# Attention scores kept in SBUF instead of computed twice, softmax sums on TensorE

## The reference

```python
xn = layernorm(x)                                        # over the 256 columns
score = einsum('bci,bcj->bij', ctx, xn) / sqrt(256)      # 64 x 256 x 256
score = softmax(score, axis=0)                           # over the 64 batches
x = x + einsum('bci,bij->bcj', ctx, score)
# then x + moe(layernorm(x)): 8 experts of 256-512-256, 2 chosen per token, gelu
```

## Time and profile before

| | |
|---|---|
| median of 3 runs | 813.24 us (811.27 to 814.58) |
| the profiled execution | 818.82 us, its span 817.0 us |
| busy share of the span | PE 91%, DVE 76%, POOL 66%, ACT 47% |
| stage 1, first to last maximum and on to stage 2 | 0 to 77 us |
| stage 2, to the first product with the reciprocal | 77 to 156 us |
| stage 3 | 156 to about 290 us |
| routing, then experts | about 290 to 346 us, then to the end |
| DMA | 137.20 MB, 174 GB/s to and from HBM over the span |

### The profile page before, as it was taken

One profiled execution on the slowest core, in us unless ns is written; L12 is line 12 of the kernel. 1 busy time (PEld: TensorE's weight loads), 2 busy tenths in 40 slices (PEclk: granted clock), 3 DMA queues, 4 the chain that ended last, 5 costly groups with the idle time before them and its releaser, 6 DMA issues. The chain is left out here.

```text
span 817.0 us, 22178 instructions
## 1 busy us (share of the span) xinstructions
PE 742.1 (91%) x5931; PEld 647.5 (79%) x5932; DVE 618.5 (76%) x1520; ACT 387.1 (47%) x716; POOL 538.5 (66%) x658
## 2 busy tenths in 40 slices
PE   6999999598999844499999999999979999999995
PEld 4777888477788734399999999999958999999995
DVE  5998999897999967786667676627467766767664
ACT  3554666375766751144444445414424444444441
POOL 4664777586888720657777777736677777777764
PEclk9999999798999955599999999979999999999998
DMA  7887876256888650445555555534355444444440
GB/s 217 259 258 233 242 234 203 88 172 207 268 270 270 228 199 0 103 141 159 183 163 186 167 181 179 160 114 132 104 167 143 152 146 134 132 139 130 139 113 1
DMA packets 82201, 137.20 MB, mean 168 GB/s; under 512 B 10075, under 2 KB 55140, under 8 KB 82032
## 3 DMA queue, kind: packets, MB, share of 16 engines
q0 software_dynamic: 23104, 68.43, 28.0%
q1 hardware_dynamic: 59056, 68.26, 26.8%
HBM read 94.56 MB, written 47.59 MB: 174 GB/s over the span
## 5 line engine op out<-in xcount | busy, mean ns | idle before, releaser
L1051 ACT ACTIVATE work<-psum,b1T 128x256 f32<-128x256 f32 x312 | 131.0, 471 | 259.3 <-PE psum L670 259.2
L670 PE MATMUL psum<-work,w1T_high 128*128 128x256 f16 x1248 | 213.1, 276 | 2.7 <-ACT work L1059 2.7
L693 PE MATMUL psum<-w2T_high,slots 128*128 x1248 | 210.2, 274 | 1.1 <-issue 1.1
L670 PE MATMUL psum<-work,w1T_low 128*128 128x256 f16 x624 | 172.3, 276 | 0.0
L693 PE MATMUL psum<-w2T_low,slots 128*128 x624 | 170.8, 274 | 0.0
L942 DVE CAST slots<-work 128x512 f16<-128x512 f32 x156 | 68.8, 441 | 118.6 <-ACT work L1051 118.4
L670 PEld LDWEIGHTS psum<-work,w1T_high 128*128 x1248 | 123.4, 99 | 18.7 <-issue 3.1
L693 PEld LDWEIGHTS psum<-w2T_high,slots 128*128 128x128 f16 x1248 | 119.2, 98 | 14.8 <-issue 1.8
L551 PE MATMUL psum<-slots,work 128*128 (+1 forms) x512 | 124.2, 393 | 7.1 <-ACT slots L981 6.5
L506 POOL DMA_INDIRECT slots<-rows_first,slots x86 | 89.4, 1039 | 60.5 <-DVE slots L903 34.6
L513 POOL DMA_INDIRECT rows_second<-slots x78 | 83.4, 1069 | 55.9 <-issue 34.7
(11 more groups left out here) (123 smaller groups left out, 1076.9 us busy)
## 6 DMA issues: line engine op xcount, KB each, us to landing
work<-in_ctx SPq DMA_DIRECT2D x96, 256.0 KB, 3.6
rows_first<-slots SPq DMA_DIRECT2D x32, 514.0 KB, 3.9
slots<-in_x SPq DMA_DIRECT2D x32, 256.0 KB, 3.8
work<-in_L_ffn_w SPq DMA_DIRECT2D x32, 256.0 KB, 3.2
work<-in_x SPq DMA_DIRECT2D x32, 256.0 KB, 3.1
slots<-rows_first,slots POOLq DMA_INDIRECT x86
rows_second<-slots POOLq DMA_INDIRECT x78
slots<-rows_second,slots POOLq DMA_INDIRECT x78, 3.7
```

Source lines behind the costliest of these rows:

```text
L670: mm = pe.matmul(h, w1T[pw][:, f, c, bass.ds(e * P, P)], xT[r2][:, (px * HC + c) * GROUP:(px * HC + c + 1) * GROUP], start=(c == 0 and px ...
L693: mm = pe.matmul(y, act16[r2][pa][:, f * GROUP + s * P:f * GROUP + (s + 1) * P], w2T[pw][:, f, bass.ds(e * DIM, DIM)], start=(f == 0 and p ...
L1051: last = act.activation(act32[r2][:, f * GROUP:(f + 1) * GROUP], psum[:, 2 + 2 * r2 + f // 2, (f % 2) * GROUP:(f % 2 + 1) * GROUP], ACT.Ge ...
```

## The change

The scores are computed once. ScalarE copies each pair's scores from PSUM into its slots, over the normalised x that TensorE has read, and VectorE takes the maximum from the same PSUM banks after that copy; the banks are now a ring of four pairs. Stage 2 has no products, ctx loads or transposes left: VectorE subtracts the maximum in SBUF, in place, ScalarE takes the exponential, and TensorE adds up by multiplying each batch's exponentials with the identity into PSUM bank 7. The reciprocal reads that bank. GpSimd does nothing in stage 2.

The host now hands over x and ctx as [row, batch, column], so that a pair is 2 KB in one piece for each partition (with 64 KB from one partition's to the next), and the expert weights, router weights and first bias already transposed. One block of 512 columns of weights is loaded, split by ScalarE and VectorE from SBUF for each pair.

```diff
@@ DMA queue (sync) @@
-            sp.wait_ge(s_setT, 1)
-            def load_exps(i, k, n):
+            def load_weights(i, k, n):
                 m, r = i + k, k % RING
-                sp.wait_ge(m_score, m + PAIRS - RING + 1)
-                sp.dma_start(ctx_ring[:, 2 * r:2 * r + 2, :], pair_of(ctx, m * 2)).then_inc(m_ctx_in[r], 16)
-                if k % 2 == 0:
...
+                after(sp, e_wlow, m - RING + 1)
+                sp.dma_start(stage[:, 2 * r:2 * r + 2, :].rearrange("p a b -> p (a b)"), weights_of(m, weights)).then_inc(e_w_in[r], 16)
@@ GpSimd: add_up and its loop are gone @@
@@ TensorE @@
+            def scores(i, k, n):
                 m, r = i + k, k % RING
                 pe.wait_ge(m_ctx_in[r], landed_at(i, k, RING))
-                after(pe, m_max, m - 1)
+                after(pe, m_max, m - RING + 1)
                 for j in range(2):
                     pe.wait_ge(m_q, m * 2 + j + 1)
...
-            pipeline(pe, PAIRS, RING, RING, 0, scores_exp)
+            def sum_up(i, k, n):
+                m = i + k
+                if isinstance(m, int) and m == 0:
+                    pe.wait_ge(m_max, PAIRS)
+                pe.wait_ge(e_exp, m + 1)
                 for j in range(2):
+                    mm = pe.matmul(psum[:, 7, :], ident[:], slot(m * 2 + j, 0, 2 * DIM), start=(isinstance(m, int) and m == 0 and j == 0),
+                                   stop=(isinstance(m, int) and m == PAIRS - 1 and j == 1))
@@ VectorE @@
                 if live(i, k, L_MAX, PAIRS):
-                    m, r2 = i + k - L_MAX, (k - L_MAX) % 2
-                    dve.wait_ge(m_score, m + 1)
-                    banks = psum[:, 2 * r2:2 * r2 + 2, :]
+                    m = i + k - L_MAX
+                    dve.wait_ge(m_kept, m + 1)
+                    banks = score_banks(k - L_MAX)
...
+            def differences(i, k, n):
                 if live(i, k, 0, PAIRS):
+                    m = i + k
+                    dve.wait_ge(m_kept, m + 1)
+                    dve.tensor_tensor(slot2(m * 2, 0, 2 * DIM), slot2(m * 2, 0, 2 * DIM),
                                       smax[:, 0:1, :].to_broadcast([P, 2, 2 * DIM]), ALU.subtract).then_inc(e_diff, 1)
+                if live(i, k, L_LOW, PAIRS):
+                    m, r = i + k - L_LOW, (k - L_LOW) % RING
+                    dve.wait_ge(e_whigh, m + 1)
+                    dve.scalar_tensor_tensor(weights_of(m, halves[1]), stage[:, 2 * r:2 * r + 2, :].rearrange("p a b -> p (a b)"), WSCALE,
+                                             weights_of(m, halves[0]), ALU.mult, ALU.subtract).then_inc(e_wlow, 1)
+            dve.wait_ge(e_sum, 1)
+            dve.reciprocal(ssum[:, 0:PROD_POOL], psum[:, 7, 0:PROD_POOL]).then_inc(e_recip, 1)
+            dve.reciprocal(ssum[:, PROD_POOL:], psum[:, 7, PROD_POOL:]).then_inc(e_recip, 1)
@@ ScalarE @@
             def queries(i, k, n):
+                if live(i, k, 0, PAIRS):
+                    m, r = i + k, k % RING
+                    act.wait_ge(m_norm, m + 1)
+                    for j in range(2):
+                        act.activation(slot(m * 2 + j, 0, DIM), slot(m * 2 + j, 0, DIM), ACT.Identity, bias=shift[:, r, j:j + 1],
+                                       scale=rstd[:, r, j:j + 1]).then_inc(m_q, 1)
+                if live(i, k, L_KEEP, PAIRS):
+                    m = i + k - L_KEEP
+                    wait_apart(act, m_score, m + 1)
+                    act.activation(slot2(m * 2, 0, 2 * DIM), score_banks(k - L_KEEP), ACT.Copy).then_inc(m_kept, 1)
+            pipeline(act, PAIRS, RING, RING, L_KEEP, queries)
...
+                act.wait_ge(e_w_in[r], landed_at(i, k, RING))
+                act.activation(weights_of(m, halves[0]), stage[:, 2 * r:2 * r + 2, :].rearrange("p a b -> p (a b)"), ACT.Copy, scale=WSCALE).then_inc(e_whigh, 1)
                 act.wait_ge(e_diff, m + 1)
                 act.activation(slot2(m * 2, 0, 2 * DIM), slot2(m * 2, 0, 2 * DIM), ACT.Exp, scale=SCORE_SCALE).then_inc(e_exp, 1)
```

More of the change, by code:

```diff
@@ L51 @@
 PR = 2 * DIM
-SUM_DVE = 128
+W_HALF = EXPERTS * HID * DIM // P
+W_STEP = 2 * W_HALF // (BATCH // 2)
 PROD_POOL = 320
@@ L130, in landed_at, with xattn_ffn @@
     return i * (16 // ring) + landed(k, ring)
-def xattn_ffn(nc, x, ctx, router_w, w1, b1, w2, b2, out):
-    w1_rows = w1.rearrange("e f h -> (e f) h")
-    w2_rows = w2.rearrange("e h f -> (e h) f")
+def xattn_ffn(nc, x, ctx, router_w, b1, weights, b2, out):
     out_rows = out.rearrange("b c l -> (b c) l")
@@ L153, in xattn_ffn @@
         slots3 = slots[:].rearrange("p (b w) -> p b w", w=ROW)
-        w1T = [sb(f"w1T_{p}", [P, FC, HC, EXPERTS * P], F16) for p in ("high", "low")]
-        w2T = [sb(f"w2T_{p}", [P, FC, EXPERTS * DIM], F16) for p in ("high", "low")]
+        halves = [sb(f"weights_{p}", [P, 2 * W_HALF], F16) for p in ("high", "low")]
+        w1T = [t[:, 0:W_HALF].rearrange("p (f h w) -> p f h w", f=FC, h=HC) for t in halves]
+        w2T = [t[:, W_HALF:].rearrange("p (f w) -> p f w", f=FC) for t in halves]
         smax = sb("smax", [P, 3, 2 * DIM])
-        sums = smax[:, 1:3, :]
-        ssum = sums[:, 0, :]
+        ssum = smax[:, 1, :]
         choice = smax[:, 0, 0:ROUNDS * BATCH].rearrange("p (r b) -> p r b", r=ROUNDS)
@@ L201, in slot2, with weights_of, score_banks @@
             return slots3[:, bass.ds(b, 2), first:first + n]
[L203 to L206 removed]
+        def weights_of(m, t):
+            return t[:, bass.ds(m * W_STEP, W_STEP)]
+        def score_banks(k):
+            return psum[:, 2 * (k % RING):2 * (k % RING) + 2, :]
         def pair_of(dram, b):
[L209 removed]
+            return dram[:, bass.ds(b, 2), :]
         s_zero = sem("s_zero")
@@ L378, in _ @@
         def _(sp):
-            sp.dma_start(rw_in, router_w).then_inc(s_rw_in, 16)
-            sp.dma_start(work[0:EXPERTS, 16:18, :].rearrange("e a b -> e (a b)"), b1).then_inc(s_b1_in, 16)
+            sp.dma_start(rwT[:].rearrange("p h e -> p (h e)"), router_w).then_inc(s_rw_in, 16)
+            sp.dma_start(b1T[:].rearrange("p e f -> p (e f)"), b1).then_inc(s_b1_in, 16)
             def load_scores(i, k, n):
@@ L391, in _ @@
             pipeline(sp, PAIRS, RING, 2 * RING, L_CTX, load_scores)
-            sp.wait_ge(s_setT, 1)
-            def load_exps(i, k, n):
+            def load_weights(i, k, n):
                 m, r = i + k, k % RING
-                sp.wait_ge(m_score, m + PAIRS - RING + 1)
-                sp.dma_start(ctx_ring[:, 2 * r:2 * r + 2, :], pair_of(ctx, m * 2)).then_inc(m_ctx_in[r], 16)
-                if k % 2 == 0:
[L401 to L405, removed]
+                after(sp, e_wlow, m - RING + 1)
+                sp.dma_start(stage[:, 2 * r:2 * r + 2, :].rearrange("p a b -> p (a b)"), weights_of(m, weights)).then_inc(e_w_in[r], 16)
+            pipeline(sp, PAIRS, RING, RING, 0, load_weights)
             def attend(i, k, n):
@@ L539, in _ @@
             pe.wait_ge(s_const, 1)
[L540 to L553, removed]
@@ L555, in scores_max @@
-            def scores_max(i, k, n):
+            def scores(i, k, n):
                 m, r = i + k, k % RING
                 pe.wait_ge(m_ctx_in[r], landed_at(i, k, RING))
-                after(pe, m_max, m - 1)
+                after(pe, m_max, m - RING + 1)
                 for j in range(2):
                     pe.wait_ge(m_q, m * 2 + j + 1)
[L561 to L569, removed]
-                for j in range(2):
[L571 to L583, removed]
@@ L584, in _ @@
-            pipeline(pe, PAIRS, RING, RING, 0, scores_exp)
+                    for h in range(HC):
+                        mm = pe.matmul(psum[:, 2 * r + j, h * DIM:(h + 1) * DIM], ctx_ring[:, 2 * r + j, h * P:(h + 1) * P], slot(m * 2 + j, 0, DIM),
+                                       start=True, stop=True)
+                mm.then_inc(m_score, 1)
+            pipeline(pe, PAIRS, RING, RING, 0, scores)
+            def sum_up(i, k, n):
[3 more added lines that the diff above has]
+                pe.wait_ge(e_exp, m + 1)
+                for j in range(2):
+                    mm = pe.matmul(psum[:, 7, :], ident[:], slot(m * 2 + j, 0, 2 * DIM), start=(isinstance(m, int) and m == 0 and j == 0),
+                                   stop=(isinstance(m, int) and m == PAIRS - 1 and j == 1))
+                if isinstance(m, int) and m == PAIRS - 1:
+                    mm.then_inc(e_sum, 1)
@@ L757, in _ @@
-            pipeline(dve, PAIRS, RING, RING, L_LOW, exponentials)
-            dve.wait_ge(e_sumv, PAIRS)
-            dve.wait_ge(e_sump, PAIRS)
-            dve.tensor_tensor(ssum, ssum, sums[:, 1, :], ALU.add).then_inc(e_total, 1)
-            dve.wait_ge(e_total, 1)
-            dve.reciprocal(ssum[:, 0:PROD_POOL], ssum[:, 0:PROD_POOL]).then_inc(e_recip, 1)
-            dve.reciprocal(ssum[:, PROD_POOL:], ssum[:, PROD_POOL:]).then_inc(e_recip, 1)
+                if live(i, k, L_LOW, PAIRS):
[3 more added lines that the diff above has]
```

(18 more changed lines are left out.)

64 lines of the change are left out of this document (11 added, 53 removed).

## The result

The changed kernel takes 816.40 us (median of 10 runs, 814.85 to 818.18) against 813.87 (median of 10, 811.27 to 815.56): a ratio of 1.0033, 95% interval 1.0018 to 1.0048. It is slower by 2.5 us or 0.3%, clear of the noise, half of the 5.2 us that were forecast, and within the 0.5% that I called no change: that outcome had 0.27, and the likelier one, slower by more, 0.57. The profiled execution took 818.18 us, with a span of 816.4.

A forecast was written before the change was run, and what follows sets the result against it. The prediction took stage 1 to be bound by a round trip through the engines, not by one engine. Stage 1 +20.3, stage 2 -15.1 and stage 3 0 gave +5.2 on 813.2, so 818.4 us; range 806 to 832.

The forecast's parts named there:

- both large terms: Stage 1 was to grow by 20.3 us and stage 2 to shrink by 15.1 us.
- The order on ScalarE sets stage 1: Stage 1: copy waits behind the next pair's normalising, so the period is 2.69 us instead of 2.04; +20.3 us in all.
- the copy: Stage 1: ScalarE's added copy of 128x1024 from PSUM per pair, taken as 1.05 us, bounds 1.0 and 1.2.
- VectorE sets stage 2's pace, TensorE its end: Stage 2: VectorE 1.74 and TensorE 1.73 us a pair, TensorE without slack for its late start; stage -15.1 us.
- The sums start at half clock: Start of stage 2's sums: after 5.6 us idle TensorE runs at half clock, losing 1.7 to 3.5 us, taken as 2.5.
- Stage 3 starts as before: Start of stage 3: TensorE again at half clock after some 3.3 us waiting; 0, with a gain of at most 1.7 us.
- The halt is not part of the median: Stage 3: VectorE's 5.0 us stop for late ctx taken as absent from the median; rival that change ends it: 813.4, 0.10.
- the clock did not fall in stage 1: Rival for stage 1: idle gaps halve TensorE's clock over half the pairs, giving 834 us; chance 0.10.
- The loads are no slower for their pitch: Rival on loads with 64 KB between partitions: twice as slow, they cost 33 us in stage 3, 851 us; chance 0.04.
- The sum on TensorE ran as said: Rival for stage 2: the sum's products take twice the 1.73 us, stage grows by 55, 874 us; chance 0.02.
- the first rival: Stage 1: the order on ScalarE doesn't bind, the period stays at 2.04 us, 799.2 us in all; chance 0.08.

The follow-up runs named there:

- the second profile of the kernel before: The kernel before, unchanged, run once more for its profile: 813.24 us in this execution.
- the half sum: The changed kernel with the second batch of each pair left out of the sums in stage 2: 810.82 us in a single execution.
- the 24 products: The changed kernel with 24 small unused identity products on TensorE between the last scores and the first sum: 813.17 us, ratio to the kernel before 1.0.
- the old layout: The changed kernel with x and ctx laid out as before, [batch, row, column] in pieces of 1 KB: 816.40 us.
- lag four: The changed kernel with VectorE's maximum taken four pairs back instead of three: 795.34 us, ratio to the kernel before 0.9785.
- the second experiment: The changed kernel with ScalarE's copy of the pair before put ahead of the normalising: 866.11 us in a single execution.

## Why the prediction was right, and where it was off

The sign, the mechanism and both large terms held. The sum of 5.2 was twice the measured 2.5, because it is a small difference of large terms, and two of them were a little too dear.

- *The order on ScalarE sets stage 1.* Shown: the loop can be read off the timeline (5.30 us for two periods against my 5.37), a lag of four frees it, and the copy ahead of the normalising makes it worse. The period in the middle of the stage is 5.30/2 = 2.65 where I had 2.69. The term that was mis-sized is the copy: 1.00 us where I took 1.05 from two copies of half the size; over 31 periods this and 0.02 elsewhere in the loop are some 1.1 us. The mean of the stage, (94.53 - 13.23)/31 = 2.62, also holds the last maximum, freed of the order as foreseen. The stage cost 19.3 us against the profile that I worked from, where I had 20.3. Against the second profile of the kernel before, whose stage 1 ends 1.0 us earlier, it cost 20.3.
- *VectorE sets stage 2's pace, TensorE its end.* Shown by the half sum. The difference from SBUF costs the same as from PSUM (1.74 a pair with the splitting, as forecast), the sums 1.73. From first difference to first product with the reciprocal it is 63.6, forecast 63.9.
- *The sums start at half clock.* Shown by the window at 0.50 and by the 24 products that end it. The cost is not fixed: without it the stretch is 157.61 - 96.45 = 61.2 us, and with it 63.6 in the kernel after, 159.06 - 96.41 = 62.7 with the old layout and 62.9 with lag four, so 1.5 to 2.4 where I had taken 2.5.
- *Stage 3 starts as before.* This step was mis-sized too: I set it to 0 with a gain of at most 1.7. TensorE idled for 3.35 us as foreseen, but the first products took 2.60 and not 3.60 us as in the earlier trace rows, since the clock fell only in the middle of them (granted 1.00 from 161 to 162 us, 0.54 in the next). With the old layout they took 3.53 and with lag four 3.33. The two seams make it up between them: from the first difference to the first addition of x it is 67.0 us in all three executions (163.52 - 96.51, 163.42 - 96.41, 141.39 - 74.38). At full clock eight such products take 1.9 (the next eight with the old layout: 1.90), so half clock cost 3.1 us over both seams in each of the three, where my terms, 2.5 and the 3.60 of the earlier trace rows, come to 4.2. It is the same stretch in the two profiles of the kernel before that was 83.4 (160.68 - 77.24) and 83.6.

```profile
76.21 1.23 DVE L746 TENSOR_TENSOR slots<-psum,smax 128x1024 f32<-128x1024 f32 x1
...
155.25 2.38 DVE L822 TENSOR_TENSOR slots<-slots,smax 128x384 f32<-128x384 f32 x2
159.81 0.69 DVE L787 TENSOR_TENSOR slots<-psum,work 128x512 f32<-128x512 f32 x1 [2.19 <-PE psum L623]
```

- *The halt is not part of the median.* Supported by the second profile of the kernel before, which has no halt and lies at the median.
- The sum, mended, up to the first addition of x: 163.52 - 160.68 = +2.8 against the first profile of the kernel before (stage 1 +19.3, the rest -16.4), 163.52 - 159.81 = +3.7 against the second (+20.3 and -16.6), and +2.5 between the medians. Single executions of the same kernel differ by 1 us in these stages and by up to 4 us in all, so the rows can't say more, and an agreement within some tenths would be luck.

The rivals: the clock did not fall in stage 1 with gaps of 0.15 to 1.35 us (granted 1.00 over the stage). It did fall with the gaps of 1.75 us in the second experiment, 0.82 in a window with 2.37 of 4 us busy. So the row that I held against this rival, 1.00 with 1.63 of 4 us busy, does not by itself speak against it. The Trainium skill (TensorE: Matmul & The Clock Gate, "A second HAM failure mode: psum-queue depth-cycling") tells of short idle times that make the clock swing; the trace of the kernel after does not agree with it, that of the second experiment does. The loads are no slower for their pitch. The sum on TensorE ran as said. And the first rival, stage 1 at its old pace, priced at 799.2, is about what one more pair of lag gives: 795.3. It also frees the 0.1 us a pair that the kernel before lost to the same loop.

## What to carry to other kernels

Before work is put on an engine that seems to have room, write the loop down: from an instruction, through every engine and every place in a queue, back to the instruction that waits, and divide by the number of iterations between them. Engine totals under the period say nothing if that quotient is larger; when it is, a deeper lag costs two lines, and here it was worth 21 us where the change itself cost 2.5. And when a hand-over leaves TensorE idle before a stage in which it has no slack (here 1.73 against VectorE's 1.74 us a pair), what the half clock costs at its start can't be made up in that stage: 24 products in the 5.6 us of idle time brought the first addition of x 2.2 us forward.

## What the runs showed of the hardware that I had not expected

Short idle times that repeat can lower TensorE's clock: with 1.75 us idle and 2.0 us busy in turn, the granted clock went from 1.00 over 0.82 to 0.50 and back, several times in the stage, while a stage with 1.99 us busy and gaps of 0.15 to 1.35 kept 1.00. The rows that I had worked from show idle time in one piece, of 3.08 and 4.29 us. The half clock behind such a piece did not fall at the same place in each execution: behind 3.35 us idle the same eight products took 2.60, 3.33 or 3.53 us. And ScalarE's copy of two PSUM banks (1.00 to 1.03 us) is no dearer than its exponential of the same shape from SBUF (1.06).
